# A transformer block on one core: row maxima transposed unsplit, their high and low parts taken behind the transposing by ScalarE and VectorE, and two rows stored by two copies

## The reference

```
x = layer_norm(hidden, ln1_w, ln1_b)
q = (x @ q_w + q_b).reshape(B, LQ, H, HD).transpose(0, 2, 1, 3)
k = (ctx @ k_w + k_b) ...  ;  v = (ctx @ v_w + v_b) ...
scores = einsum('bhqd,bhkd->bhqk', q, k) * scale
scores = where(mask, scores, finfo.min)
out = einsum('bhqk,bhkd->bhqd', softmax(scores), v)
hidden = out @ cproj_w + cproj_b + hidden
y = gelu(layer_norm(hidden, ln2_w, ln2_b) @ fc_w + fc_b)
out = hidden + y @ proj_w + proj_b
```

## Time and profile before

| | us |
|---|---|
| median of 3 executions | 764.95 |
| lowest and highest of them | 764.66, 768.26 |
| the profiled execution's own time | 765.3 |
| its span in the profile | 763.5 |
| TensorE busy in the span | 703.7 |
| VectorE busy | 460.8 |
| ScalarE busy | 322.2 |
| GpSimd busy | 251.0 |

### The profile page before, as it was taken

How to read it: one execution, slowest core, us unless ns; L and a number is a source line. 1 busy time by engine, 2 the same in 40 slices (tenths; PEclk the granted TensorE clock), 3 DMA queues, 4 the chain that set the end, 5 groups by cost and what they waited for, 6 DMA issues and landing times.

```text
span 763.5 us, 13145 instructions
## 1 busy us (share of the span) xinstructions
PE 703.7 (92%) x4544; PEld 610.1 (80%) x4544; DVE 460.8 (60%) x860; ACT 322.2 (42%) x581; POOL 251.0 (33%) x217
## 2 busy tenths in 40 slices
PE   4489989899998989999889999999999999999998
PEld 3378879798888889888667888888888888888886
DVE  5367978988788897978877766442325223151213
ACT  4237766867676686757652121112211121211110
POOL 3505656655545665655752212000000001000000
PEclk9788989999999999999889999999999999999999
DMA  9756554644455464434604500010001000010001
GB/s 247 203 139 176 160 159 123 166 138 154 139 153 153 124 168 111 135 103 143 180 30 125 165 1 1 0 56 1 2 0 56 0 0 0 0 55 1 1 0 57
DMA packets 51130, 69.16 MB, mean 91 GB/s; under 512 B 8328, under 2 KB 29192, under 8 KB 51088
## 3 DMA queue, kind: packets, MB, share of 16 engines
q1 hardware_dynamic: 50816, 68.07, 30.8%
q0 software_dynamic: 272, 0.54, 0.4%
HBM read 47.21 MB, written 20.99 MB: 89 GB/s over the span
## 4 chain that ended last, share of the span: by engine, by line
PE 68%; issue 10%; POOL 6%; DVE 5%; DMA 4%; SPq 3%; ACT 3%; DVEq 0%; ACTq 0%; POOLq 0%
PE psum L1172 8%; PE psum L1174 8%; PE psum L1173 8%; PE psum L1159 7%; PE psum L1157 7%; PE psum L1158 7%; PE psum L975 5%; PE psum L977 5%; PE psum L976 5%; POOL p_lo L462 5%; PE psum L1009 2%; DMA stacks<-qk_rows 2%; PE psum L1059 2%; DMA qk_rows<-qk 2%; PE psum L993 1%
## 5 line engine op out<-in xcount | busy, mean ns | idle before, releaser
L462 POOL TENSOR_TENSOR p_lo<-p,p_hi 128x512 f16<-128x512 f32 x128 | 156.0, 1228 | 137.6 <-ACT p_hi L535 137.3
L662 ACT ACTIVATE h<-psum,cols 128x512 f32<-128x512 f32 x64 | 44.1, 690 | 290.0 <-PE psum L1159 290.0
L913 DVE CAST h_hi<-h 128x512 fp32r<-128x512 f32 x64 | 27.6, 432 | 207.3 <-ACT h L662 207.3
L533 ACT ACTIVATE p<-psum,maskbias 128x512 f32<-128x512 f32 x128 | 88.3, 690 | 47.2 <-PE psum L993 46.1
L1172 PE MATMUL psum<-w_mlp,h_hi 128*128 128x512 f32 x256 | 100.7, 393 | 0.9 <-DVE hidden L758 0.9
L1174 PE MATMUL psum<-w_mlp,h_lo 128*128 128x512 f32 x256 | 99.7, 390 | 0.0
L1173 PE MATMUL psum<-w_mlp,h_hi 128*128 128x512 f32 x256 | 99.7, 390 | 0.0
L1157 PE MATMUL psum<-y_hi,w_mlp 128*128 128x512 f32 x256 | 99.7, 389 | 0.0
L1159 PE MATMUL psum<-y_hi,w_mlp 128*128 128x512 f32 x256 | 99.7, 389 | 0.0
L1158 PE MATMUL psum<-y_lo,w_mlp 128*128 128x512 f32 x256 | 99.6, 389 | 0.0
L535 ACT ACTIVATE p_hi<-psum,maskbias 128x512 f16<-128x512 f32 x128 | 88.8, 694 | 0.0
(11 more groups left out here) (104 smaller groups left out, 1514.2 us busy)
## 6 DMA issues: line engine op xcount, KB each, us to landing
qk_rows<-qk SPq DMA_DIRECT2D x32, 512.0 KB, 2.7
stacks<-qk_rows SPq DMA_DIRECT2D x64, 256.0 KB
stacks<-qk_rows SPq DMA_DIRECT2D x64, 128.0 KB
hidden<-in_x_dram SPq DMA_DIRECT2D x8, 512.0 KB, 4.4
ctx_sb<-in_ctx_dram SPq DMA_DIRECT2D x8, 512.0 KB, 5.3
w_mlp_raw<-in_L_xattn_fc_w_dram SPq DMA_DIRECT2D x16, 256.0 KB, 4.5
w_mlp_raw<-in_L_xattn_proj_w_dram SPq DMA_DIRECT2D x16, 256.0 KB, 6.2
out_dram<-hidden SPq DMA_DIRECT2D x16, 256.0 KB, 2.1
```

The costliest lines, as they stand in the source:

```text
L462: pool.tensor_tensor(p_lo[:, slot, :], p32[:, u % 2, :], p_hi[:, slot, :], ALU.subtract).then_inc(s["p_lo_done"], 1)
L533: act.activation(p32[:, u % 2, :], psum[:, ST + kc, :], ACT.Exp, bias=maskbias[:, kc:kc + 1], scale=SCALE32)
```

## The change

The maxima are transposed as they are, four columns instead of twelve, from two `negm` buffers in turn. ScalarE copies the four PSUM rows into `mrow` rows 0 to 3 (the rounding makes them the high part). VectorE subtracts these from the PSUM rows into `mrow` rows 32 to 35 (`maxima_lo`). SyncE stores each in a DMA of its own, into stack rows 96 and 97. The cast L736, the subtraction L738 and the memsets of `m12` and of the stacks' k rows go. The mask moves to row 98, and the fill of each group now writes three rows (two fixed ones, q zero and k one, and the mask row) out of `mask_rows`, which is filled at the start by two stores instead of one. The first pass of the scores takes 99 rows instead of 97, the second 98 instead of 99. The bank of the transposed maxima is free when the low part is done, not when ScalarE has copied. In step 1 the second half of the attention output's transposes moves behind `values`, and its high and low parts behind the second exponentials and behind the products.

```
@@ -60,8 +60,8 @@
     MASKED = float(2.0 ** 127)
-    MAXROWS = 3 * HD + 1
-    SUBROWS = 3 * HD + 3
+    MAXROWS = 3 * HD + 3
+    SUBROWS = 3 * HD + 2
     SCALE32 = float(np.float32(SCALE))
@@ -110,13 +110,13 @@
 att = sb("att", [P, TT, D], fp32, A4)
+fixed_rows = sb("fixed_rows", [B, 2, 2, LK], fp32, A4)
 vb_bc = sb("vb_bc", [P, D], fp32, A4 + 4 * KB)
...
 A5 = A4 + 8 * KB
-negm = sb("negm", [P, TT, GH], fp32, A5)
-m12 = sb("m12", [P, TT, 3 * GH], fp32r, A5 + 32)
+negm = [sb(f"negm{i}", [P, TT, GH], fp32, A5 + 32 * i) for i in range(2)]
 rl = sb("rl", [P, TT, H], fp32, A5 + 160)
-mrow = sb("mrow", [3 * GH, LQ], fp32r, A5 + 288)
+mrow = sb("mrow", [HD + GH, LQ], fp32r, A5 + 288)
 mrow_raw = sb("maskrow_raw", [B, LK], u8, A5 + 288 + KB)
@@ -134,7 +134,7 @@
-mask_rows = nc.dram_tensor("mask_rows", [B, 2, LK], fp32, kind="Internal").ap()
+mask_rows = nc.dram_tensor("mask_rows", [B, 3, 2, LK], fp32, kind="Internal").ap()
 qk_rows = nc.dram_tensor("qk_rows", [2, P, 4 * LQ], fp32, kind="Internal").ap()
@@ -194,7 +194,7 @@
             return None
-        return ("qk_lo_done", (G + 1) * 2) if kind == "qk" else ("mrow_ready", G + 1)
+        return ("qk_lo_done", (G + 1) * 2) if kind == "qk" else ("m_lo_done", G + 1)
     b = it + {"v": 1, "att": -1, "c": -1 - n, "x": 2, "ctx": 1}[kind]
@@ -320,8 +320,9 @@
     sp.wait_ge(s["pool_consts"], 5)
-    sp.dma_start(mask_rows, maskrow[:, :, :]).then_inc(s["mask_stored"], 16)
-    sp.wait_ge(s["mask_stored"], 16)
+    sp.dma_start(mask_rows[:, 2], maskrow[:, :, :]).then_inc(s["mask_stored"], 16)
+    sp.dma_start(mask_rows[:, 0:2], fixed_rows[:, :, :, :]).then_inc(s["mask_stored"], 16)
+    sp.wait_ge(s["mask_stored"], 32)
@@ -341,16 +342,19 @@
             address_follows()
-            wait(sp, "mrow_ready", G - 1)
-            sp.dma_start(qst[3 * HD:3 * HD + 3, slot, :].bitcast(fp32),
-                         mrow[:, :].bitcast(fp32)).then_inc(s["m_stored"], 16)
+            wait(sp, "m_hi_done", G - 1)
+            sp.dma_start(qst[3 * HD:3 * HD + 1, slot, :].bitcast(fp32),
+                         mrow[0:GH, :].bitcast(fp32)).then_inc(s["m_stored"], 16)
+            wait(sp, "m_lo_done", G - 1)
+            sp.dma_start(qst[3 * HD + 1:3 * HD + 2, slot, :].bitcast(fp32),
+                         mrow[HD:HD + GH, :].bitcast(fp32)).then_inc(s["m_stored"], 16)
         if group(G):
...
             row = mask_rows[b:b + 1] if isinstance(b, int) else mask_rows[bass.ds(b, 1)]
-            sp.dma_start(stacks[3 * HD:3 * HD + 1, slot, :, :].bitcast(fp32),
-                         row.rearrange("b (o n) q -> b o n q", o=1).to_broadcast([1, GH, 2, LK])).then_inc(filled, 16)
+            sp.dma_start(stacks[3 * HD:3 * HD + 3, slot, :, :].rearrange("r h n q -> r h (n q)").bitcast(fp32),
+                         row.rearrange("b r (o n) q -> (b r) o (n q)", o=1).to_broadcast([3, GH, 2 * LK])).then_inc(filled, 16)
             address_follows()
@@ -416,12 +420,10 @@
     pool.wait_ge(s["pool_consts"], 1)
-    pool.memset(m12[:, :, :].bitcast(fp32), 0.0).then_inc(s["pool_consts"], 1)
     pool.memset(vparts[:, :, :, 0:1], 1.0).then_inc(s["pool_consts"], 1)
     pool.memset(maskrow[:, 0, :], 1.0).then_inc(s["pool_consts"], 1)
-    pool.wait_ge(s["pool_consts"], 4)
-    pool.memset(kst[3 * HD:3 * HD + 3, :, :].bitcast(fp32), 1.0).then_inc(s["pool_consts"], 1)
-    pool.wait_ge(s["pool_consts"], 5)
+    pool.memset(fixed_rows[:, :, 0, :], 0.0).then_inc(s["pool_consts"], 1)
+    pool.memset(fixed_rows[:, :, 1, :], 1.0).then_inc(s["pool_consts"], 1)
@@ -570,15 +572,14 @@
             wait(act, "m_tr", G + 1)
-            wait(act, "m_stored", G * 16)
-            act.activation(mrow[:, :], in_bank("m", g)[0:3 * GH, 0:LQ], ACT.Copy).then_inc(s["mrow_ready"], 1)
-
-    def attention_hi(b):
+            wait(act, "m_stored", G * 32)
+            act.activation(mrow[0:GH, :], in_bank("m", g)[0:GH, 0:LQ], ACT.Copy).then_inc(s["m_hi_done"], 1)
+
+    def attention_hi(b, j):
         wait(act, "c_proj", b * 2)
-        for j in range(2):
-            wait(act, "att_tr", b * 2 + (j + 1))
-            act.activation(att_t[:, 0, 2 * j:2 * j + 2, :], in_bank("att", j).rearrange("p (k q) -> p k q", k=2),
-                           ACT.Copy).then_inc(s["att_hi_done"], 1)
+        wait(act, "att_tr", b * 2 + (j + 1))
+        act.activation(att_t[:, 0, 2 * j:2 * j + 2, :], in_bank("att", j).rearrange("p (k q) -> p k q", k=2),
+                       ACT.Copy).then_inc(s["att_hi_done"], 1)
@@ -627,8 +628,10 @@
             if batch(it - 1):
-                attention_hi(it - 1)
+                attention_hi(it - 1, 0)
             exps(it, g, 1)
+            if batch(it - 1):
+                attention_hi(it - 1, 1)
         if g == 2:
@@ -724,18 +727,18 @@
         if heads[0] == 0:
-            wait(dve, "m_lo_done", G)
+            wait(dve, "m_tr", G - 1)
         for h in heads:
...
             wait(dve, "max_mm", n + 1)
-            dve.tensor_reduce(out=negm[:, :, h:h + 1], in_=psum[:, MX + h % 2, :].rearrange("p (t k) -> p t k", t=TT),
+            dve.tensor_reduce(out=negm[g % 2][:, :, h:h + 1], in_=psum[:, MX + h % 2, :].rearrange("p (t k) -> p t k", t=TT),
                               axis=AX.X, op=ALU.max, negate=True).then_inc(s["max_taken"], 1)
-        if heads[-1] == GH - 1:
-            wait(dve, "max_taken", (G + 1) * 4)
-            wait(dve, "m_tr", G)
-            dve.tensor_copy(m12[:, :, GH:2 * GH], negm[:, :, :]).then_inc(s["m_hi_done"], 1)
+
+    def maxima_lo(it, g):
+        G = it * NG + g + 1
+        if group(G):
             wait(dve, "m_hi_done", G + 1)
-            dve.tensor_tensor(m12[:, :, 2 * GH:3 * GH], negm[:, :, :], m12[:, :, GH:2 * GH].bitcast(fp32),
+            dve.tensor_tensor(mrow[HD:HD + GH, :], in_bank("m", g)[0:GH, 0:LQ], mrow[0:GH, :].bitcast(fp32),
                               ALU.subtract).then_inc(s["m_lo_done"], 1)
@@ -798,6 +801,11 @@
+    def attention_lo(b, j):
+        wait(dve, "att_hi_done", b * 2 + (j + 1))
+        dve.tensor_tensor(att_t[:, 1, 2 * j:2 * j + 2, :], in_bank("att", j).rearrange("p (k q) -> p k q", k=2),
+                          att_t[:, 0, 2 * j:2 * j + 2, :].bitcast(fp32), ALU.subtract).then_inc(s["att_lo_done"], 1)
+
     def products_out(it, g):
@@ -805,6 +813,7 @@
             wait(dve, "att_tr", it * 2)
+            wait(dve, "mask_stored", 32)
         for t in range(TT):
@@ -836,7 +845,11 @@
             products_out(it, g)
+        if g == 3:
+            maxima_lo(it, g)
         maximum(it, g, (0, 1))
+        if g != 3:
+            maxima_lo(it, g)
         if g == 0 and batch(it + 1) and not (isinstance(it, int) and it == -1):
@@ -846,13 +859,11 @@
         if g == 1 and batch(it - 1):
-            b = it - 1
-            for j in range(2):
-                wait(dve, "att_hi_done", b * 2 + (j + 1))
-                dve.tensor_tensor(att_t[:, 1, 2 * j:2 * j + 2, :], in_bank("att", j).rearrange("p (k q) -> p k q", k=2),
-                                  att_t[:, 0, 2 * j:2 * j + 2, :].bitcast(fp32), ALU.subtract).then_inc(s["att_lo_done"], 1)
+            attention_lo(it - 1, 0)
         if g == 1:
             products_out(it, g)
+        if g == 1 and batch(it - 1):
+            attention_lo(it - 1, 1)
         if g == 2 and batch(it + 2):
@@ -984,7 +995,7 @@
         if pair == 0:
-            wait(pe, "m_stored", (G + 1) * 16)
+            wait(pe, "m_stored", (G + 1) * 32)
         for kc in range(KC):
@@ -1001,7 +1012,6 @@
             wait(pe, stack_filled[g % 2], fills_upto(G, g % 2))
-            wait(pe, "pool_consts", 5)
         for hh in heads:
@@ -1087,10 +1097,10 @@
             return
-        wait(pe, "m_lo_done", G + 1)
+        wait(pe, "max_taken", (G + 1) * 4)
         bank = bank_of(it, "m", g)
         for t in range(TT):
-            ins = nc.tensor.transpose(bank[0:3 * GH, t * P:(t + 1) * P], m12[:, t, :].bitcast(fp32), ident[:, :])
+            ins = nc.tensor.transpose(bank[0:GH, t * P:(t + 1) * P], negm[(g + 1) % 2][:, t, :], ident[:, :])
         ins.then_inc(s["m_tr"], 1)
@@ -1115,9 +1125,9 @@
             scores(it, g, (0, 1))
-            for j in range(2):
-                transposes(it, "att", j, it - 1, att, "att_normed", 2, "att_tr")
+            transposes(it, "att", 0, it - 1, att, "att_normed", 2, "att_tr")
             values(it, g)
+            transposes(it, "att", 1, it - 1, att, "att_normed", 2, "att_tr")
             project_v(it, 0)
```

More of the change, by code:

```diff
@@ L159, in xattn_kernel @@
             qk_proj x_tr ctx_tr max_mm st_mm pv_mm m_tr att_tr v_proj c_proj
-            x_affine_act x_affine_dve qk_hi_done qk_lo_done p_hi_done p_lo_done mrow_ready att_hi_done att_lo_done
+            x_affine_act x_affine_dve qk_hi_done qk_lo_done p_hi_done p_lo_done att_hi_done att_lo_done
             v1_cast v_cast v_rest v_split v_added max_taken m_hi_done m_lo_done pv_taken att_normed hidden_added
@@ L545, in first_part @@
             def first_part(b):
-                wait(act, "mask_stored", 16)
```

(1 more changed line is left out.)

## The result

The changed kernel takes 775.06 us (median of 4 executions, 773.0 to 780.07), the kernel before 766.61 beside it (4 executions, 764.66 to 770.21). The ratio is 1.0126, with a 95% interval of 1.0091 to 1.0161: slower. It is estimated over all the executions; the quotient of the two medians is 1.0110. The forecast was 777, slower, range 766 to 788. The profiled execution took 773.0, 771.2 of it in the span, 7.7 more than the span of before.

The account below looks back on a forecast made before the run. TensorE was taken to set the pace, busy 703.7 of 763.5 us. Terms 4.2 + 2.0 + 4.0 + 0.4 + 1.7 = 12.3 on the profiled 765.3 gave 777.6, less 0.35 for the median, about 777; range 766 to 788.

Parts of the forecast that it names:

- The wait that is to go: Step 1, TensorE's transposes of the maxima waiting 1.69 us for VectorE's subtraction: gain taken as 0, other end 2 us.
- Step 0's loads: Stack loads behind SyncE's low-part wait issue 2.03 us later, slack 1.19: scores wait 0.84, +4.2 us in 5 iterations.
- Step 2's loads and `add_hidden`: Step 2's loads nearly without slack, `add_hidden` pushed on VectorE: +0.5 us in about 4 iterations, +2.0.
- The edges: First and last attention iterations and existing load waits: some four places where later loads cost, +4 us, bounds 1 and 7.
- The clock: TensorE's clock in attention: longer pauses bring one more dip to 1.2 GHz, +1.7 us, bounds 0 and 8.3.
- The start: Kernel start, two mask stores instead of one ahead of the context load: +0.4 us, bounds 0 and 1.
- no-change case: Rival over the whole kernel: cheap stores, loads landing as before, subtraction hidden; 763 to 768, mid 765; chance 0.12.

Follow-up runs that it names:

- e3: Kernel before, with the maxima's store cut in two and SyncE waiting between them for the step's first pair of maxima: 771.61 us, ratio 1.0074.
- e4: Changed kernel, with VectorE taking the low part earlier, ahead of the first pair of maxima in step 0 and the products in step 3: 770.21 us, ratio 1.0065.
- e8: Kernel before, with TensorE's scores of heads 0 and 1 ahead of the transposes of the maxima in step 1: 763.9 us, ratio 0.9975.
- e10: e8 with SyncE issuing the mask row's fill ahead of its wait for ScalarE: 764.01 us, ratio 0.9943 to the kernel before.
- e1: Changed kernel, with SyncE issuing mask fill and stack loads ahead of its wait for the low part and the second store: 781.6 us, ratio 1.0203.
- e7: e4 with TensorE's scores of heads 0 and 1 ahead of the transposes of the maxima in step 1: 769.65 us, ratio 1.0041 to the kernel before.
- e9: e7 with the high part's store on ScalarE's queue and the three-row fill ahead of SyncE's low-part wait: 768.47 us, ratio 1.0013 to the kernel before.
- e12: Changed kernel, with the low part taken early (ahead of the products) in step 3 alone: 774.96 us, ratio 1.0091 to the kernel before.
- e5: Kernel before, with a second 4x256 subtraction added on VectorE and the transposed maxima's bank held until it is done: 779.94 us, ratio 1.0187.

## Why the prediction was right

The direction and the time hold, 777 forecast and 775.06 measured, and the cause it named, late loads, is a good half of the loss (e3). That the time came so near is partly luck, as the steps show:

- *The wait that is to go*: gain taken as 0. The wait at the transposes fell by 1.26 in each iteration, and two others came ahead of it and behind it, so the sum was right. The place where VectorE's added time comes out was not: it is not the last pair of maxima, which starts only 0.16 later, it is `x_lo`, 0.82 at the projection. From the transposes of step 0 to those of step 1 it is 9.95 us after (191.20 to 201.15), 10.20 before (184.35 to 194.55).
- *Step 0's loads*: forecast 0.84 in each of 5 iterations, 4.2 in all; the waits are 0.86, 1.06, 0.74, 0.76 and 0.29, 3.7 in all. The low part ends 3.74 behind the transposes of step 0 (191.20 to 194.94), 3.70 in the forecast (184.35 to 188.05). The issues were cheaper than taken: a store with its gap 0.78 instead of 1.02 (194.97 to 195.75), the fill with its gap 0.43 instead of 0.80. The first load came 1.42 later against the first store, not 2.03. But the loads took longer, see below, and the sum came out.
- *Step 2's loads and `add_hidden`*: forecast +0.5 in each of four iterations, 2.0 in all; measured +0.6 in the one shown (13.36 to 13.97) and 1.4 in four, with both waits in the rows: 0.74 for the loads, then 0.30 for `add_hidden`.
- *The edges*: forecast +4, measured +6.6 (5.0, 1.0 and 0.6), with the fifth of the iterations, which the steady window leaves out, counted in. The term was undersized, and its mechanism only half named. The late loads are in it (0.69); but the first iterations also lose to the bank of the x transposes, which the low part now frees (1.93), and to the fall of the clock behind it. This is the step that failed.
- *The clock*: forecast +1.7, a cost. At the start of the attention it was one, in the stretch that takes 5.0 more: busy time grew by 1.2 there. Over the four steady iterations it was a gain: the clock rose from 0.97 to 1.00, about 1.6 us for each of three falls. The forecast had pauses that are longer in sum bring more falls; what the change did was to break one pause of 1.69 into three with work between them. In e3, where the pause stays whole and the waits for the loads are as after, the clock is 0.95. In e4, with the broken pause, it is 1.00 over the like stretch:

```profile
148.00:321.70 173.70, 160.95 (x1474) 146.29 (x1472) 139.75 (x264) 121.56 (x221) 98.31 (x85) 1.00 0.51 144
```

That a broken pause is what keeps the clock up fits these two, but it is not shown, and it is not a rule that other runs bear out: in e8 the clock fell behind 1.09 and 0.34, and in e10 it is 0.77 over 195.0 to 199.5, behind 0.67 and 0.34.

- *The start*: forecast +0.4; the transposes of the first group come at 46.5 instead of 46.7 us. Too small to tell.

So the steady part was forecast at +7.9 for five iterations and gave +1.4 over four, because there the clock's sign was wrong; the edges were forecast at 4 and gave 6.6. An iteration was to grow by 1.3 us and grew by 0.35 on the average. Two errors of opposite sign make the total look better than its parts. (The lower end of the range, 766, is called the middle of the no-change case, which the prediction itself puts at 765; nothing hangs on it.)

The prediction also cited the Trainium skill, page SBUF — State Buffer, section Who interferes with whom, on VectorE instructions with one and with two SBUF inputs. In line with it, the new subtraction takes 412 to 416 ns in all 32 places. `x_lo`, with two SBUF inputs, grew from 1.60 to 2.05, and that growth isn't in the prediction. The first `x_lo`, where GpSimd computes nothing, takes 1.20. It takes 2.0 in all eight kernels here that have a subtraction on VectorE in step 0 (the change, e1, e4 to e7, e9, e12), and 1.6 in the six that have none. GpSimd's pair of instructions starts 2.68 us behind the transposes of step 0 in both kernels, `x_lo` 3.22 before and 3.78 after. Before, the pair is stretched to 3.04; after, it takes 2.06, and `x_lo` is the one that is stretched. That GpSimd's work at that moment is the cause is argued from this, not shown by an experiment.

Three things stay open: why the scores in step 1 start 6.41 us behind the first load's issue (196.18 to 202.59), where 5.70 was taken from another step; what the removed cast and subtraction are worth alone; and how what e3 leaves of the loss, about 0.5%, is shared between the bank, `x_lo` and the clock.

## What to carry to other kernels

A wait put into a queue that issues DMAs delays all that stands behind it in the queue: ask what those transfers have as slack, in time from issue to use, before asking how long the wait is. And a shared bank that is freed by a later instruction of a busy engine moves that engine's order into the bound one's (1.2 us an iteration in e5): look up who uses the bank next. Last, judge a repaired change against a base with the same repairs: e9 looks like no loss beside the kernel before, and like 0.7% beside e10.

## What the runs showed of the hardware

- TensorE's granted clock fell to the lower level behind an unbroken pause of 1.69 us in three of four steady iterations of the kernel before (not in each: the earlier trace rows), and in none of four of the changed kernel behind pauses of 0.82, 0.43 and 1.06 with work between them, though their sum is larger. One such fall cost 1.6 us (11.63 against 10.03). Shorter and broken pauses are no guarantee: in e8 it fell behind 1.09 and 0.34 once and stayed up behind 1.06 and 0.34. What decides is not shown here.
- A DMA that fills three partitions with 24 KB issues in 0.38 us (0.29 to 0.45), the one that fills one partition with 8 KB in 0.66, and the store of q and k, 128 partitions of 4 KB, in 0.34. The issue time doesn't follow size.
- The same VectorE subtraction with two SBUF inputs, 1024 elements in each of 128 partitions, takes 1.20 us where GpSimd computes nothing, and 1.60 or 2.05 beside it, as the rows of step 0 show: where it started 0.56 us later against GpSimd's pair, it took 0.45 more and the pair 1.0 less.
